# Feed-forward alternated by chunk, its first pass begun on half a pair, half the output stored from SyncE, and z's weights loaded first

## The reference

```python
# block 1: a gated recurrence over the 256 steps, then 8 experts, top 2 of them per token
gate = sigmoid(h @ Wh.T + z_t @ Wz.T + b);  h = tanh(h * (1 - alpha) + gate * z_t)
h1 = relu(xt @ w1[e] + b1[e]);  out_e = h1 @ w2[e] + b2[e]        # chosen experts summed
x = x + out
# block 2: a mixture (shared expert + 8 routed ones, top 2), then a quantised feed-forward
y = (shared + routed) / 3
def quant_act_uint8(v):  s = max(max(v), EPS) / 255;  return clip(round(v / s), 0, 255) * s
h = relu(quant_act_uint8(y) @ w1q.T + b1q)                         # w1: 1024 x 256
x = x + quant_act_uint8(h) @ w2q.T + b2q                           # w2: 256 x 1024
```

## Time and profile before

| | us |
|---|---|
| median of 3 runs | 1263.15 (1262.4 to 1264.03) |
| profiled execution, its own time | 1267.8 |
| its span | 1264.8 |
| TensorE busy | 1123.6 |
| VectorE busy | 892.9 |
| ScalarE busy | 583.3 |
| GpSimd busy | 250.9 |

### The profile page before, as it was taken

One profiled execution on the slowest core, in us unless ns is written; L12 is line 12 of the kernel. 1 busy time (PEld: TensorE's weight loads), 2 busy tenths in 40 slices (PEclk: granted clock), 3 DMA queues, 4 the chain that ended last, 5 costly groups with the idle time before them and its releaser, 6 DMA issues.

```text
span 1264.8 us, 32645 instructions
## 1 busy us (share of the span) xinstructions
PE 1123.6 (89%) x10732; PEld 864.7 (68%) x10733; DVE 892.9 (71%) x3002; ACT 583.3 (46%) x1782; POOL 250.9 (20%) x289
## 2 busy tenths in 40 slices
PE   6777777787768999999999999889999999987895
PEld 4665666565557999998899999746766666763263
DVE  5677677676775587965555555468898889987875
ACT  3555555555553444444444444362445533434373
POOL 1002112112114675343333333300000000001001
PEclk9999999999999999999999999989999999998998
DMA  6222333233233475343333333243000000000035
GB/s 174 76 72 89 90 97 97 82 93 109 71 91 106 102 166 133 91 70 59 58 53 60 62 62 62 36 132 134 2 1 1 0 1 0 1 1 1 1 51 83
DMA packets 57527, 84.36 MB, mean 67 GB/s; under 512 B 7361, under 2 KB 47170, under 8 KB 57410
## 3 DMA queue, kind: packets, MB, share of 16 engines
q1 hardware_dynamic: 41186, 57.94, 16.1%
q0 software_dynamic: 16224, 24.96, 10.9%
HBM read 51.36 MB, written 35.70 MB: 69 GB/s over the span
## 4 chain that ended last, share of the span: by engine, by line
PE 75%; ACT 9%; DVE 9%; issue 3%; DMA 1%; SPq 1%; POOL 0%; DVEq 0%; ACTq 0%; POOLq 0%
PE ps L570 23%; PE ps L1105 16%; PE ps L1117 16%; PE ps L1660 7%; DVE ps L1589 5%; PE ps L1665 4%; ACT work L1516 4%; ACT ps L1511 3%; DVE imax L986 2%; PE ps L924 2%; PE ps L1630 1%; PE ps L1086 1%; ACT W L955 1%; PE ps L1638 1%; PE ps L911 1%
## 5 line engine op out<-in xcount | busy, mean ns | idle before, releaser
L1141 ACT ACTIVATE lane<-ps,b_now 128x256 f32<-128x256 f32 x312 | 147.4, 474 | 240.1 <-PE ps L1105 216.4
L1105 PE MATMUL ps<-lane,W 128*128 128x256 f16 x1872 | 213.3, 274 | 2.2 <-ACT lane L1129 1.3
L1117 PE MATMUL ps<-W,lane 128*128 x1872 | 210.7, 273 | 0.0
L1105 PEld LDWEIGHTS ps<-lane,W 128*128 x1872 | 184.0, 98 | 25.1 <-issue 2.8
L1117 PEld LDWEIGHTS ps<-W,lane 128*128 128x128 f16 x1872 | 181.5, 98 | 20.4
L1660 PE MATMUL ps<-work 128*128 128x16 f16 x2048 | 99.1, 177 | 89.5 <-ACT work L1516 88.8
L1660 PEld LDWEIGHTS ps<-work 128*128 128x128 f16 x2048 | 76.3, 107 | 141.3 <-ACT work L1516 139.9
L1284 POOL DMA_INDIRECT results<-lane,dest x78 | 123.8, 1588 | 231.3 <-DVE lane L1198 195.8
L570 PE MATMUL ps<-W,work 128*128 128x512 f16 x768 | 168.7, 382 | 0.0
L1210 DVE TENSOR_TENSOR lane<-lane 128x256 f16<-128x256 f32 x312 | 133.4, 427 | 10.8
L570 PEld LDWEIGHTS ps<-W,work 128*128 128x128 f16 x768 | 74.9, 98 | 90.1 <-issue 2.2
(11 more groups left out here) (214 smaller groups left out, 1533.7 us busy)
## 6 DMA issues: line engine op xcount, KB each, us to landing
lane<-rows SPq DMA_DIRECT2D x39, 257.0 KB
stage<-in_w1T SPq DMA_DIRECT2D x16, 512.0 KB, 3.7
stage<-in_w2T SPq DMA_DIRECT2D x16, 512.0 KB, 4.0
b_now<-in_b SPq DMA_DIRECT2D x39, 128.0 KB
work<-in_zT SPq DMA_DIRECT2D x32, 128.0 KB, 2.2
results<-in_xn SPq DMA_DIRECT2D x32, 128.0 KB
W<-results SPq DMA_DIRECT2D x8, 512.0 KB, 3.8
out<-W SPq DMA_DIRECT2D x8, 512.0 KB, 4.9
```

Source lines behind the costliest of these rows:

```text
L1105: last = pe.matmul(ps[:, f % 4, 0:ST], of_e(W1[:, bass.ds(e, 1), a, k, f * P:(f + 1) * P]), xT[:, p, b, k], start=(i == 0 and k == 0), sto ...
L1117: last = pe.matmul(ps[:, 4 + q, 0:D], hid[:, a, f, q * P:(q + 1) * P], of_e(W2[:, bass.ds(e, 1), b, f]), start=(i == 0 and f == 0), stop=( ...
L1141: act.activation(v4[:, f % 4], ps[:, f % 4, 0:ST], ACT.Relu, bias=b1_now[:, p, f:f + 1], scale=A_SCALE / W_SCALE).then_inc(l1_v, 1)
```

## The change

1. **SP's loads at the start** come in another order: `WT`, z tile 0, `b_row`, `h0`, `alpha`, `gw`, the two expert pieces, z tiles 1 to 3, the small tables. Three semaphores replace one, so that DVE starts on `WT` alone and PE on `wz` alone; `gw` is split after the first `rest`.
2. **The last group's largest value** is taken by two 512-wide reductions, the first between the additions.
3. **First pass.** `row_max` starts its first chunk when the first group of the pair is there, and the transposes are spread: two before pair 0, then one after chunk 2 and one after chunk 5 of pairs 0 to 2. ACT copies groups 0 and 1 out before it quantises group 2.
4. **Second pass.** PE alternates chunk by chunk: `hidden(g + 1, f)`, then the four products of chunk `f` of group `g`. The wait on `ob_s` stands ahead of both. The last group does its two halves one after the other. The loop is gone, all 8 groups are written out.
5. **Output.** Groups 4 to 7 are no longer stored ahead and accumulated: DVE adds the bias to `x1` of these groups (`x_with_bias`, four 1024-wide additions after the casts of group 1), writes the result into `y`, and SP stores it in 8 plain DMAs of 256 KB. POOL accumulates groups 0 to 3 as before.

```diff
@@ mixture, DVE
+                        if is_last(g) and p == E // 2 - 1:
+                            dve.wait_ge(y_acc, YG * g + acc_index(p, q2 + 1, 1) + 1)
+                            dve.tensor_reduce(ymax[:, g + q2 // 2:g + q2 // 2 + 1],
+                                              y[:, GT * g + q2:GT * g + q2 + 2].rearrange("p q d -> p (q d)"),
+                                              AX.X, ALU.max).then_inc(ymax_in, 1)
@@ feed-forward, PE
             def row_max(n):
-                pe.wait_ge(yq_T, 2 * n + 2)
+                pe.wait_ge(yq_T, 2 * n + 1)
                 for f in range(FC):
...
                     for m in range(2):
+                        if f == 0 and m == 1:
+                            pe.wait_ge(yq_T, 2 * n + 2)
...
+                    if f in (2, 5) and 2 * n + 2 + f // 5 < GROUPS:
+                        transposes(2 * n + 2 + f // 5)
...
             def group(g, buf):
-                if not is_last(g):
-                    hidden(g + 1)
                 if not is_tile(g, 0) and not is_tile(g, 1):
                     pe.wait_ge(ob_s, 2 * (g - 1))
-                for q in range(GT):
+                if is_last(g):
+                    for half in range(2):
+                        for f in range(FC):
+                            if half == 0:
+                                wait_rounded(pe, g, f)
+                            for q in (2 * half, 2 * half + 1):
+                                last = output(buf, f, q)
+                        last.then_inc(ob_ps, 1)
+                else:
                     for f in range(FC):
-                        if q == 0:
-                            wait_rounded(pe, g, f)
...
+                        hidden(g + 1, f)
+                        wait_rounded(pe, g, f)
+                        for q in range(GT):
+                            last = output(buf, f, q)
@@ feed-forward, DVE
+                th = y[:, GT * g + 2 * half:GT * g + 2 * half + 2] if stored_here else xh
...
+            def x_with_bias(g):
+                xg_ = x1[:, GT * g:GT * g + GT]
+                dve.tensor_tensor(xg_, xg_, bq2.rearrange("p (a d) -> p a d", a=1).broadcast_to([P, GT, D]), ALU.add)\
+                   .then_inc(xb_ready, 1)
...
                 if not is_last(g):
                     hidden(g + 1, 1 - buf, None if is_tile(g, 0) else (g - 1, 1 - buf))
+                    if is_tile(g, 0):
+                        dve.wait_ge(bq_ready, 3)
+                        for k in range(ADDED, GROUPS):
+                            x_with_bias(k)
@@ output, SP
-            for g in range(GROUPS):
+            for g in range(ADDED):
                 sp.dma_start(out[:, GT * g:GT * g + GT], x1[:, GT * g:GT * g + GT]).then_inc(x_out, 16)
...
+            for n in range(2 * ADDED, 2 * GROUPS):
+                sp.wait_ge(ob, n + 1)
+                sp.dma_start(out[:, 2 * n:2 * n + 2], y[:, 2 * n:2 * n + 2]).then_inc(last_out, 16)
@@ start, DVE and PE
-            dve.wait_ge(w_in, 64)
+            dve.wait_ge(w_in, 16)
             dve.wait_ge(prep, 1)
...
-            pe.wait_ge(prep, 8)
+            pe.wait_ge(prep, 2)
             pe.wait_ge(z_in[0], 16)
+            for part in range(3 * DC):
+                if part == 2:
+                    pe.wait_ge(prep, 5)
+                z_part(0, part)
             pe.wait_ge(idents, 11)
-            for part in range(3 * DC):
-                z_part(0, part)
+            pe.wait_ge(gw_split, 2)
```

More of the change, by code:

```diff
@@ L837, in mix @@
                                    .then_inc(y_acc, 1)
-                dve.wait_ge(y_acc, YG * g + YG)
-                dve.tensor_reduce(ymax[:, bass.ds(g, 1)], y[:, bass.ds(GT * g, GT)].rearrange("p q d -> p (q d)"),
-                                  AX.X, ALU.max).then_inc(ymax_in, 1)
+                        if is_last(g) and p == E // 2 - 1:
[3 more added lines that the diff above has]
+                                              AX.X, ALU.max).then_inc(ymax_in, 1)
+                if not is_last(g):
+                    dve.wait_ge(y_acc, YG * g + YG)
+                    dve.tensor_reduce(ymax[:, bass.ds(g, 1)], y[:, bass.ds(GT * g, GT)].rearrange("p q d -> p (q d)"),
+                                      AX.X, ALU.max).then_inc(ymax_in, 1)
             mix_groups(dve, mix)
         def ffn_groups(eng, group):
-            for g in (0, 1):
-                group(g, g)
-            with eng.Fori(1, GROUPS // 2 - 1) as i:
-                group(2 * i, 0)
-                group(2 * i + 1, 1)
-            for g in (GROUPS - 2, GROUPS - 1):
+            for g in range(GROUPS):
                 group(g, g % 2)
@@ L894, in ffn_pe @@
             largest(0)
-            for n, groups in enumerate((range(0, 3), range(3, 6), range(6, 8), ())):
-                for g in groups:
-                    transposes(g)
+            for g in range(2):
+                transposes(g)
+            for n in range(GROUPS // 2):
                 row_max(n)
@@ L904, in ffn_pe, with hidden @@
             pe.wait_ge(ia_mx, FC * GROUPS // 2)
-            def hidden(g):
-                for f in range(FC):
-                    if not (is_tile(g, 0) and f < 4):
-                        pe.wait_ge(hb_h, FC * g + f - 3)
-                    for k in range(DC):
-                        last = pe.matmul(ps[:, f % 4], w1qT[:, k, f * P:(f + 1) * P], yqT[:, k, bass.ds(GN * g, GN)],
-                                         start=(k == 0), stop=(k == DC - 1))
-                    last.then_inc(hb_ps, 1)
+            def hidden(g, f):
+                if not (is_tile(g, 0) and f < 4):
+                    pe.wait_ge(hb_h, FC * g + f - 3)
+                for k in range(DC):
+                    last = pe.matmul(ps[:, f % 4], w1qT[:, k, f * P:(f + 1) * P], yqT[:, k, bass.ds(GN * g, GN)],
+                                     start=(k == 0), stop=(k == DC - 1))
+                last.then_inc(hb_ps, 1)
@@ L929, in ffn_pe @@
-            hidden(0)
+                if is_last(g):
[7 more added lines that the diff above has]
+                else:
+                    for f in range(FC):
+                        hidden(g + 1, f)
+                        wait_rounded(pe, g, f)
+                        for q in range(GT):
+                            last = output(buf, f, q)
+                            if f == FC - 1 and q % 2:
+                                last.then_inc(ob_ps, 1)
@@ L930, in ffn_pe @@
+            for f in range(FC):
+                hidden(0, f)
             ffn_groups(pe, group)
@@ L938, in ffn_act, with quantised @@
             act.wait_ge(inv_ready, 1)
[L939 removed]
+            def quantised(g):
                 act.activation(y8[:, g], y[:, GT * g:GT * g + GT].rearrange("p q d -> p (q d)"), ACT.Relu,
                                scale=inv[:, 0:1]).then_inc(yq_m, 1)
[L942 to L944 removed]
+            for g in range(GROUPS):
+                quantised(g)
+                if g == 1:
+                    transposed(0)
+                if g == 1 or g >= 3:
+                    transposed(g if g == 1 else g - 1)
             transposed(GROUPS - 1)
@@ L1339, in _, with load_w @@
         def _(sp):
+            def load_w(i, j):
+                src = (w1T, w2T)[j // 2][bass.ds(i, 1)].rearrange("a p n -> p (a n)")
+                sp.dma_start(stage[:, j % 2], src[:, 1024 * (j % 2):1024 * (j % 2) + 1024]).then_inc(piece_in[j % 2], 16)
             sp.dma_start(wst, WT).then_inc(w_in, 16)
-            sp.dma_start(h0[:], h0T).then_inc(w_in, 16)
-            sp.dma_start(alpha[:], alphaT).then_inc(w_in, 16)
+            sp.dma_start(z[:, 0], zT[:, 0]).then_inc(z_in[0], 16)
             sp.wait_ge(const0, 1)
-            sp.dma_start(b_mat[0:1, :], b_row).then_inc(w_in, 16)
-            for j in range(RING):
+            sp.dma_start(b_mat[0:1, :], b_row).then_inc(b_in, 16)
+            sp.dma_start(h0[:], h0T).then_inc(h_in, 16)
+            sp.dma_start(alpha[:], alphaT).then_inc(h_in, 16)
+            sp.dma_start(gw[:], gate_wT).then_inc(gw_in, 16)
+            for j in range(2):
+                load_w(0, j)
+            for j in range(1, RING):
                 sp.dma_start(z[:, j], zT[:, j]).then_inc(z_in[j], 16)
-            sp.dma_start(gw[:], gate_wT).then_inc(gw_in, 16)
             sp.dma_start(gb_row[:], gate_b.broadcast_to([P, E])).then_inc(small_in, 16)
@@ L1369, in next_z @@
                 sp.dma_start(z[:, j], zT[:, RING * i + j + RING]).then_inc(z_in[j], 16)
-            for j in range(2):
-                load_w(0, j)
             sp.wait_ge(zeroed, 2)
@@ L1571, in _ @@
             dve.tensor_tensor(h_lo, h0[:], h_hi, ALU.subtract).then_inc(lo_ready, 1)
+            dve.tensor_scalar(alpha[:], alpha[:], -2.0, 2.0, ALU.mult, ALU.add).then_inc(prep, 1)
+            dve.wait_ge(prep, 6)
             def rest(h, j, c):
```

62 lines of the change are left out of this document (33 added, 29 removed).

## The result

| | before | after |
|---|---|---|
| median, us | 1263.52 (1262.4 to 1264.03, 4 runs) | 1250.22 (1249.42 to 1251.9, 4 runs) |
| ratio after / before | | 0.9898, 95% interval 0.988 to 0.9915 |
| profiled execution, and its span | 1267.8, 1264.8 | 1250.51, 1248.7 |

The spans differ by 16.1, but 2.6 of that is the recurrence behind its first steps (357.2 before, 354.6 after), which the change doesn't touch. So I compare stretches and not whole spans.

What follows compares the result with a forecast made beforehand. PE held 75% of the wait chain, DVE bounding the first pass and PE the second. Terms -2.6 + 0.1 - 3.1 + 0.3 - 3.1 = -8.4 took the median from 1263.15 to 1254.8 us, range 1251.0 to 1259.5.

Steps and rivals of the forecast that it cites:

- The output part: End of kernel: SP's last plain store lands 2.7 after DVE's end instead of 5.8, -3.1 us.
- 5.6 of closing work: End of span: 5.6 us follow the last store's landing, and the forecast left them unchanged.
- Start, -2.6: Start: step 0 2.5 earlier, 0.5 from the expert piece, 0.4 lost on z tile 1; sum -2.6 us, from -1.7 to -3.3.
- The term that was too small: Start, before step 1: z tile 1, issued behind both expert pieces, lands late and costs +0.4 us, between 0 and 1.
- Largest value, +0.1: Last group's largest value: two half-width reductions hide nothing and wait twice for the last addition, +0.1 us, -0.1 to +0.2.
- First pass, -3.1: First pass: reductions start 2.0 earlier, idle time inside 1.9 instead of 3.0; -3.1 us, from -2.2 to -3.6.
- Second pass, +0.3: Second pass: alternation gains 0.5 per group, but DVE's wide additions stall PE 3.2 ahead of group 2; net +0.3 us.
- its 16 switches leave gaps: Second pass rival: gaps of 0.03 at PE's layer switches take back 0.5 per group, time 1258; within a shared chance of 0.16.
- the rival of the falling clock: Second pass: the 3.2 stall drops the clock, about 4 of work at half speed, 2.0 lost, 1256.8 us; chance 0.25.
- The rival without a wait: Second pass: PE is never held ahead of group 2, 1251.6 us; chance 0.08.
- the one of a late release in every group: Second pass, groups 2 to 7: late `ob_s` release costs 1.4 each, 8.4 in all, making the kernel slower; chance 0.04.
- The Trainium skill's price of a GpSimd DMA: Output: 2.0 us fixed plus bytes at 436 GB/s; by it the output part is worth 0.6 and the forecast 1257.3.

Runs made afterwards that it cites:

- the start alone: The kernel before with only the new load order, semaphores and DVE order at the start; 1262.34 us, ratio 0.9986.
- the first pass alone: The kernel before with only the new first pass and the largest value in two halves; 1259.06 us, ratio 0.9961.
- The second pass alone: The kernel before with only PE's chunk alternation and the loop written out, all eight groups still accumulated; 1260.29 us, ratio 0.9971.
- the output alone: The kernel before with groups 4 to 7 stored by SP, four additions on DVE and the loop written out, PE's order unchanged; 1254.60 us, ratio 0.9923.

## Why the prediction was wrong

**The output part, the failed step.** "The span ends at 1264.8, so 5.6 of closing work follow the landing; I leave these as they are." I took the 5.6 for something every program does at its end. It belonged to POOL: 4.97 of it is the drain after its last accumulating store, and the change puts SP's store last. After, 0.4 follows the landing. That is 5.2 of the 5.8 by which the part was too small (8.94 instead of 3.1). The other 0.6 is the landing, 2.0 where I took 2.4, and an issue that follows DVE's end at once. The row was in the trace of before: a drain that starts at 1259.6 on POOL, when DVE's own, of 0.73, had started at 1252.7. The runs with 7, 6 and 5 groups accumulated move the drain across the end and the end follows it, 8.69, 5.67, 2.45, the last of these set by SP.

**Start, -2.6.** Step 0 came 2.22 earlier (2.5 forecast), as DVE's first operation waited on `WT` until 4.38 and not 4.2. The wait for `stage` is gone (0.78, where I took 0.5), and PE waits 0.87 to 1.32 for z tile 1. By step 8 the pair of profiles shows -2.6, the sum as forecast, but that is luck. In the profile of after the granted clock happened to be at full from 8.4 to 11.8, where two products of z tile 1 took 0.49 instead of 0.79 or 0.80 as in all the others, and the wait ahead of them was the shortest of all. The others have step 8 at 20.8 to 21.2 with the new start and at 23.0 to 23.5 with the old one, some -2.1, and timed alone it was -1.8. The term that was too small is z tile 1: taking its wait away gave 0.9 by step 8, where I had put its cost at 0.4.

**Largest value, +0.1.** It is too small to be read in any run.

**First pass, -3.1 against -4.0.** The first reduction comes 6.23 after the end of the operation that makes the scale (6.1 forecast, 8.1 before), 6.38 and 8.25 by the table: -1.87. The idle time inside fell from 3.0 to 0.8, not to 1.9. A spread transpose has a row of 0.61, but the products behind it start 0.44 after it (1143.38, 1143.82), and the second PSUM pair lets PE be late by part of a reduction before DVE sees it (that part is read from the code). I had charged each at its row's length. The clock also rose sooner than I had assumed, 10.2 after its fall instead of 13.7; no run tells apart what that gave.

**Second pass, +0.3 against +1.6.** The alternation alone saved 2.99 (2.9 forecast); that its 16 switches leave gaps falls as a rival. The wait ahead of group 2 was there, at the place and with the releaser named, 2.74 instead of 3.2: the additions took 4.62 (4.6 forecast) and the way from there to the release 3.9 (4.1). Then **the rival of the falling clock came true**: the granted clock was at half for 3.4, and the second pass is 4.6 longer than without the wait, of which 2.74 are the wait and 1.9 the rest (2.0 forecast). I had given it 0.25, since the wait "may end just before"; it ended at 2.74 and the clock fell all the same, in both profiles. The Trainium skill ("TensorE: Matmul & The Clock Gate", on oscillation) warns of such gaps between bursts of products. It gives the direction and the trace agrees, but the waits of its example are longer than this one, so it could not settle whether a wait of some 3 was enough; only the trace did. The rival without a wait didn't happen, nor the one of a late release in every group: it stood only once.

**The Trainium skill's price of a GpSimd DMA** ("DMA: Bandwidth & Descriptors", on one DMA's anatomy) put the accumulating store at 3.2 and the new one at 2.6, both by estimate. The first landed in 5.4 to 5.7 and the second in 2.0. The section is about DMAs issued by GpSimd, and the new store is SP's, so the second estimate stretched it. The 0.6 that followed for the output part were further off than my 3.1, and what mattered, the drain, is in neither.

**The sum.** By stretches it is -2.1 - 4.0 + 1.6 - 8.9 = -13.4, against -13.3 (-15.2 to -10.7) measured. The forecast's -8.4 missed 5.8 of the output and 0.9 of the first pass, and lacked a loss of 1.3 in the second and of 0.5 in the start. What a run takes beyond its span changed too, which I had taken as fixed. In the 34 runs of before that were timed beside the experiments it is 2.1 in the median (1.8 to 3.8), and it scatters as well with the start alone (1.8 to 3.3) and the first pass alone (1.8 to 3.6). In all 40 runs of the other kernels, after among them, it is 1.8 or 1.9. So 0.3 of the gain in the medians lies outside the span. The second pass alone and the output alone share one edit, the loop written out, so it goes with that; why is open. The change as it is written also gives some of its gain away: spread over four groups, the additions give back 4.6, and z tile 1 one place earlier 0.9.

## What to carry to other kernels

Read the last 10 us of a profile by engine, closing instructions too: a store's own landing may be half of what stands there, and the other half may belong to the engine that issued it, so that another engine's store ends the program at once. A batch of small operations put into a queue costs the consumer behind it their sum; one in each period costs nothing where the engine has that much idle time. Parts that were measured alone don't add where one takes the slack that the other needs.

## What the runs showed of the hardware

- **POOL's drain grows with its stores.** It took 4.65, 4.73, 4.81, 4.89 and 4.97 us with 4, 5, 6, 7 and 8 accumulating stores of 512 KB, the same to 0.01 in each repeat: 0.082 per store, which leaves 4.32 for a kernel without such stores, by extrapolation. All of them also have the 142 indirect DMAs of the earlier stages, so the base may be theirs; this was not tried. SP's drain takes 7 ns after 8 plain stores.
- **A cast on DVE takes as long as the POOL addition that it starts beside.** Four additions of 128 x 1024 32-bit elements took POOL 2.46 to 2.52 each. The four casts of 128 x 512 from bytes to 16 bits that started beside one took 2.56 or 2.57 instead of 0.42, one cast per addition. What POOL's additions take without DVE beside them was not tried.
- **The clock falls after a wait of 2.74.** It was at half for 3.4 after the wait, with PE busy from the first moment. At the head of the first pass it is down for 13.6 or 13.7 in the five profiles with the old first pass and for 10.2 or 10.3 in the nine with the new one.
- **The granted clock of the recurrence can't be taken from the page's row.** In the profile of after the row has it at half from 11.8 to 384, in its repeat at full (mean 0.84 and 0.989). But PE's products there have the same lengths in both, 0.42 and 0.56, and so they have in before. Only in the stretch from 8.4 to 11.8 of after, at full in the record, do they take 0.28 at the least. So the recurrence ran at the lower level (1.2 of 2.4 GHz) in all three, whatever the row says, and the means near 0.99, that of before too, are too high by that stretch. That is worked out from the lengths of the products. It took 354.62 and 354.72. PE waits for ACT and DVE in every step there; no run has more than two of its steps at full speed, so what the clock costs it is not shown. The page's clock row of after, and its products of z tiles by line, in the recurrence of after, of its repeat, and in the stretch at full:

```profile
PEclk6555555555558999999999999979999999998999
L1677 PE MATMUL ps<-work x240: 421/491/561, 20.0 to 359.2; 128*128 128x128 f32 x120
L1677 PE MATMUL ps<-work x240: 421/491/562, 20.8 to 360.1; 128*128 128x128 f32 x120
L1677 PE MATMUL ps<-work x4: 275/316/377, 9.4 to 10.2; 128*128 128x128 f32 x4
```

- **Steps of the recurrence of 2.1 instead of 1.43.** There were four in the profile of before and none in after, none to four in the others; with none of them the recurrence takes 354.3 to 354.7. One of them, in the timeline of before:

```profile
128.70 0.28 PE L1665 MATMUL ps<-work 128*128 128x16 f16 x4
...
129.71 0.18 ACT L1511 ACTIVATE ps<-ps 128x32 f32<-128x32 f32 x1 [1.10 <-PE ps L1665]
```

  The product that ACT waits for was done at 128.98, and ACT starts 0.7 later for no reason that the profile shows. Together they move a span by up to 2.8. All 13 of them, in five of the 14 profiles, fall on the same step of a batch of 32: number 82, 114, 146, 178, 210 or 242, counted from 0. So the step is fixed, and chance decides only in which batches it shows. The cause stays open.
